# The gates of the routing stage by token halves, with part of the path weighting moved between them

## What is computed

```python
outs = [local_out, mid_out, delta_out, v_direct]
...
router_feat = jnp.concatenate([hidden_states] + feats, axis=-1)
h1 = jax.nn.silu(router_feat @ r_w1 + r_b1)
logits = (h1 @ r_w2 + r_b2).reshape(B, L, H, 4)
p = jax.nn.softmax(logits, -1)
p = p * (1.0 - 4.0 * FLOOR) + FLOOR
mixed = sum((p[..., i:i + 1] * outs[i] for i in range(4)))
rms = jnp.sqrt(jnp.mean(mixed * mixed, -1, keepdims=True) + EPS_MIX)
mixed = mixed / rms * mix_w
```

## Time and profile before

| | us |
|---|---|
| median of three runs | 8313.55 (8311.75 to 8318.34) |
| time of the profiled execution | 8321.09 |
| its span, first to last instruction | 8319.4 |
| TensorE busy | 7418.7 (89%) |
| VectorE busy | 4851.6 (58%) |
| ScalarE busy | 3369.7 (41%) |
| mean granted TensorE clock | 0.942 of full speed |

### The profile page before, as it was taken

One profiled execution on the slowest core, in us unless ns is written; L12 is line 12 of the kernel. 1 busy time (PEld: TensorE's weight loads), 2 busy tenths in 40 slices (PEclk: granted clock), 3 DMA queues, 4 the chain that ended last, 5 costly groups with the idle time before them and its releaser, 6 DMA issues. The chain is left out here.

```text
span 8319.4 us, 123018 instructions
## 1 busy us (share of the span) xinstructions
PE 7418.7 (89%) x48014; PEld 4312.9 (52%) x48014; DVE 4851.6 (58%) x9364; ACT 3369.7 (41%) x6883; POOL 1774.6 (21%) x2690
## 2 busy tenths in 40 slices
PE   6899988999889898899898998988999889998898
PEld 3546455464554645546455464554645546455464
DVE  5465654656646566565665646656466564666546
ACT  2252432525325253352533525335253442534425
POOL 2212221122211212112221122211222121221121
PEclk9999999999999999999999999999999999999999
DMA  3021210112112021120211202112021210212102
GB/s 73 18 34 28 37 41 21 33 25 37 41 23 43 13 37 41 28 40 15 32 41 29 39 15 32 41 34 44 6 32 41 37 41 6 32 41 37 41 10 33
DMA packets 337771, 268.59 MB, mean 32 GB/s; under 512 B 213521, under 2 KB 276369, under 8 KB 337097
## 3 DMA queue, kind: packets, MB, share of 16 engines
q1 hardware_dynamic: 337148, 260.09, 16.7%
HBM read 48.71 MB, written 42.02 MB: 11 GB/s over the span
## 5 line engine op out<-in xcount | busy, mean ns | idle before, releaser
L1814 DVE TENSOR_REDUCE sa_nm<-ps 128x2 f32<-128x1024 f32 (+4 forms) x1280 | 1393.5, 1115 | 388.9 <-PE ps L1799 198.5
L1889 ACT ACTIVATE pre<-ps 128x512 f32<-128x512 f32 (+3 forms) x3072 | 1272.3, 491 | 743.3 <-PE ps L1877 737.8
L1877 PE MATMUL ps<-sa_qs,sa_ks 99*128 99x512 bf16 (+3 forms) x3072 | 806.8, 337 | 136.6 <-DMA sa_qs<-sa_mrow 72.6
L1795 PE MATMUL ps<-sa_ks,sa_qs 96*128 96x512 bf16 (+3 forms) x2560 | 660.6, 332 | 82.8 <-DVE sa_nm L1814 68.9
L1896 POOL TENSOR_SCALAR_AFFINE_SELECT pre<-pre 128x512 f32<-128x512 f32 x512 | 325.0, 635 | 1766.6 <-ACT pre L1889 1764.2
L1909 PE MATMUL ps<-pre,sa_va 128*17 128x512 f32 (+3 forms) x6144 | 644.8, 491 | 8.2 <-POOL pre L1896 8.2
L1877 PEld LDWEIGHTS ps<-sa_qs,sa_ks 99*128 99x128 bf16 x3072 | 259.3, 98 | 715.8 <-ACT pre L1889 473.8
L318 PE MATMUL ps<-identb 128*128 128x512 bf16 x2320 | 583.2, 398 | 10.5 <-ACT dr_z L1153 10.5
L705 PE MATMUL ps<-rep,stack 128*32 128x512 f32 x4608 | 530.9, 613 | 33.7 <-DMA rep<-paths 33.7
L949 POOL TENSOR_TENSOR A<-paths 128x256 f32<-128x256 f32 x384 | 268.0, 726 | 792.3 <-DVE paths L1119 792.3
L1795 PEld LDWEIGHTS ps<-sa_ks,sa_qs 96*128 96x128 bf16 x2560 | 248.8, 101 | 269.0 <-DVE sa_nm L1814 98.5
(11 more groups left out here) (364 smaller groups left out, 14154.2 us busy)
## 6 DMA issues: line engine op xcount, KB each, us to landing
sa_qs<-sa_parts SPq DMA_DIRECT2D x288, 128.0 KB, 4.5
sa_ks<-sa_parts SPq DMA_DIRECT2D x288, 128.0 KB, 5.9
x<-in_x SPq DMA_DIRECT2D x17, 1024.0 KB, 5.6
rep<-paths SPq DMA_DIRECT2D x128, 128.0 KB, 2.7
bounce<-paths SPq DMA_DIRECT2D x32, 512.0 KB, 2.9
out_y<-x SPq DMA_DIRECT2D x32, 512.0 KB, 3.0
rep<-paths SPq DMA_DIRECT2D x128, 127.9 KB, 2.6
rep<-paths SPq DMA_DIRECT2D x128, 127.8 KB, 3.4
```

Of the source, the lines that this page charges most:

```text
L1795: last = nc.tensor.matmul(cols[:, i, :], qs[0:NCOMB * AD, g % NBUF, op.j + i, op.t * P:(op.t + 1) * P], ks[0:NCOMB * AD, g % NBUF, op.j + ...
L1814: nc.vector.tensor_reduce(nm[:, g % 2, op.c, op.t, op.j:op.j + op.heads], cols, AX.X, ALU.max, negate=True).then_inc(s.slot_free, 1)
L1877: last = nc.tensor.matmul(bank[:, off:], ks[0:QROWS, g % NBUF, j, kt * P:(kt + 1) * P], qs[0:QROWS, g % NBUF, j, n * BANK + off:(n + 1) * ...
L1889: nc.scalar.activation(pt[:, gs % 2, j, off:BANK], ring_bank(ring_use(gs, j))[:, off:], ACT.Exp, scale=RATIO).then_inc(s.ring_out, 1)
```

## The change

The softmax is made for one token half at a time, on VectorE and on ScalarE. `gather_logits_of(0)` moves up, behind unit 7 instead of behind unit 9, and raises `logits` for its half. After the first half's gates VectorE weights paths 0 to 2 of that half inside `route`, then copies the second half's partial logits, weights path 3 of the first half, and makes the second half's gates. A new semaphore, `read`, tells TensorE that the first half's logits have been read from their PSUM bank. In `mix_and_project` only the second half's four weightings remain, and `mix(0, ...)` waits for none. The diff, cut to its core:

```diff
+def weigh_path(nc, m, i, n):
+
+    tn, gn = T // NB, T * H // NB
+    path = (m.local_tm, m.mid_tm, m.delta_tm, m.v_tm)[i][:, n * tn:(n + 1) * tn, :].rearrange("p t (h d) -> p (t h) d", h=H)
+    return nc.vector.tensor_tensor(path, path, m.prob[:, n * gn:(n + 1) * gn, i:i + 1].to_broadcast([P, gn, DH]), ALU.mult)
...
-                act.wait_ge(s.shifted, 1)
-                nc.scalar.activation(lg[:].rearrange("p n c -> p (n c)"), lg[:].rearrange("p n c -> p (n c)"),
-                                     ACT.Exp).then_inc(s.exp, 1)
+                for n in range(NB):
+                    act.wait_ge(s.shifted, n + 1)
+                    nc.scalar.activation(lg[:, groups(n), :], lg[:, groups(n), :], ACT.Exp).then_inc(s.exp, 1)
...
                 for n in range(NB):
+                    tiles, half = slice(n * (BANK // P), (n + 1) * (BANK // P)), groups(n)
                     dve.wait_ge(s.partial_ps, n + 1)
                     nc.vector.tensor_copy(partial[:, n * BANK:(n + 1) * BANK], ps[:, PARTIAL[n], :]).then_inc(s.partial, 1)
...
+                    if n:
+                        weigh_path(nc, m, PATHS - 1, 0)
+                    dve.wait_ge(s.logits, n + 1)
...
+                    dve.wait_ge(s.read, n + 1)
+                    settle(nc.vector.tensor_reduce(red[:, half], lg[:, half, :], AX.X, ALU.max))
+                    nc.vector.tensor_tensor(lg[:, half, :], lg[:, half, :], bc(red[:, half], PATHS), ALU.subtract).then_inc(s.shifted, 1)
+                    dve.wait_ge(s.exp, n + 1)
...
+                    gates = nc.vector.tensor_scalar(m.prob[:, half, :], lg[:, half, :], 1.0 - PATHS * FLOOR, FLOOR, ALU.mult, ALU.add)
+                    if n == 0:
+                        settle(gates)
+                        for i in range(PATHS - 1):
+                            weigh_path(nc, m, i, 0)
...
                 def gather_logits_of(n):
                     pe.wait_ge(s.partial, n + 1)
+                    if n:
+                        pe.wait_ge(s.read, n)
...
-                    return last
+                    last.then_inc(s.logits, 1)
...
                     if u == HC + 1:
                         partial_logits_of(0)
-                gather_logits_of(0)
+                    if u == HC + 2:
+                        gather_logits_of(0)
                 partial_logits_of(1)
-                gather_logits_of(1).then_inc(s.logits, 1)
+                gather_logits_of(1)
...
-                for n in range(NB):
-                    for i in range(PATHS):
-                        nc.vector.tensor_tensor(of(paths[i], n), of(paths[i], n),
-                                                m.prob[:, n * GN:(n + 1) * GN, i:i + 1].to_broadcast([P, GN, DH]),
-                                                ALU.mult).then_inc(s.part, 1)
+                for i in range(PATHS):
+                    weigh_path(nc, m, i, 1).then_inc(s.part, 1)
...
-                        pe.wait_ge(s.part, PATHS * n + i + 1)
+                        if n:
+                            pe.wait_ge(s.part, i + 1)
```

More of the change, by code:

```diff
@@ L1191, in route, with groups @@
         partial = sb("ro_partial", [P, L])
+        def groups(n):
+            return slice(n * (T * H // NB), (n + 1) * (T * H // NB))
         def feature(first, n):
@@ new lines, in _ @@
+                    dve.wait_ge(s.logits, n + 1)
+                    nc.vector.tensor_tensor(lg[:, half, :].rearrange("p (t h) c -> p t (h c)", h=H),
+                                            ps[:, 6, 0:T * H * PATHS].rearrange("p (t n) -> p t n", t=T)[:, tiles],
+                                            k.rb2[:].unsqueeze(1).to_broadcast([P, BANK // P, H * PATHS]), ALU.add).then_inc(s.read, 1)
+                    dve.wait_ge(s.read, n + 1)
+                    settle(nc.vector.tensor_reduce(red[:, half], lg[:, half, :], AX.X, ALU.max))
@@ new lines, in _ @@
+                    nc.vector.tensor_tensor(lg[:, half, :], lg[:, half, :], bc(red[:, half], PATHS), ALU.subtract).then_inc(s.shifted, 1)
+                    dve.wait_ge(s.exp, n + 1)
+                    settle(nc.vector.tensor_reduce(red[:, half], lg[:, half, :], AX.X, ALU.add))
+                    settle(nc.vector.reciprocal(red[:, half], red[:, half]))
+                    settle(nc.vector.tensor_tensor(lg[:, half, :], lg[:, half, :], bc(red[:, half], PATHS), ALU.mult))
+                    gates = nc.vector.tensor_scalar(m.prob[:, half, :], lg[:, half, :], 1.0 - PATHS * FLOOR, FLOOR, ALU.mult, ALU.add)
@@ L2169 @@
           "x_ps x10 t01 t23 y6_ps y6 t_ps t6 kq attn ks r u_ps u s_ps state o o_out",
-    "ro": "feats ft_ps ft h1_ps h1 partial_ps partial logits shifted exp",
+    "ro": "feats ft_ps ft h1_ps h1 partial_ps partial logits read shifted exp",
     "mi": "part mixed square kept summed scale_in scale wide spread ot out",
```

## The result

The changed kernel is slower: 8395.04 us median against 8315.94, a ratio of 1.0089 (95% interval 1.0073 to 1.0105). That is 79 us or 4.9 us for each of 16 sequences, where 43 us had been forecast (2.7 a sequence), and above the range, which ended at 8384. The profiled execution has a span of 8393.0 against 8319.4, 4.6 us a sequence.

What follows compares the result with a forecast made beforehand. TensorE, busy 89% of the span, was taken as the bound, so gains must come from its idle time. Terms 1.65 + 0.2 + 0.4 + 0.45 gave 2.7 us for each of 16 sequences, +43 us: 8356, range 8326 to 8384.

Steps and rivals of the forecast that it cites:

- Steps 1 to 3: First half's gates in routing: last Silu 1.11 us later, Exp done at 287.32, VectorE reaches first weighting at 288.38.
- step 1: Gathering of the first half ahead of units 8 and 9: the last Silu ends 1.11 us later.
- Step 4: Three weightings ahead of the second copy on VectorE, 3.44 us: the copy ends 3.35 us later.
- Steps 6 to 8: Second half's gates take 2.03 us, mix starts net 1.65 later; two sequences lose their fast partial logits, averaged +0.2.
- Step 9: Second gathering on TensorE, after a longer idle time, runs at a lower clock: +0.4 us, bounds nothing and +1.1.
- steps 1 to 9: Everything up to the start of the mix: 1.65 + 0.2 + 0.4 us later in each sequence.
- Step 10: Mix restarts at clock 0.50 with a low stretch at least as long: +0.45 us, bounds -1.9 and +2.0.
- A: The terms as summed: +43 us, 8356, own range 8335 to 8370; chance 0.60.
- D: Low stretch of the mix twice as long and second gathering slow: 4.9 us a sequence, +79 us, 8393; chance 0.22.
- B: Clock stays at 1.00 across the gap before the mix, saving 1.9 us: 8313, half of it 8328; chance 0.13.
- C: Second copy isn't held up by the three weightings and the kernel is faster, 8302 to 8271; chance 0.05.
- step 2: First half's Exp on ScalarE waits for ten Silus and a 1.28 us table load, ending at 287.32.

Runs made afterwards that it cites:

- both edits: Changed kernel with paths 2 and 3 weighted in the mix block, one weighting before the second copy, first gathering behind the last unit: 8355.80 us, ratio 1.0044.

## Why the prediction was wrong

**Bound and prize (what bounds the kernel).** Right: TensorE's gap ahead of the mix, of which moving weightings could take 1.28 us. They took it: the mix starts with its block.

**Steps 1 to 3.** Right. The last Silu ends 4.64 us behind the first copy (forecast 4.57), the Exp of the first half at 6.21 (6.09), with no pause behind the table load, and the first weighting starts at 7.27 (7.15). The run with the gathering late shows the chain from step 1 on. The further 1.38 us that I had worked out from the Trainium skill, ScalarE: Activation LUTs, section "What ACT_TABLE_LOAD costs", didn't appear here either: the load ends at 286.32 and the Exp starts at 286.33.

**Step 4, the queue.** Right: second copy at 10.68, forecast 10.59. The run with the copy early takes 2.7 us off the start of the mix.

**Steps 6 to 8.** Right: 2.06 us of gates (2.03), 0.30 for the meeting, and the two fast sequences have lost their lead, all 16 start the mix at 15.7 to 16.0.

**Step 9, clock of the second gathering.** Right mechanism, wrong size: 1.89 instead of 1.07 us, 0.8 where I took 0.4. The weighting beside it had ended by 292.9, 0.8 before the logits, and hid nothing of the excess. With this the start of the mix is 2.69 later against 2.25 forecast in steps 1 to 9 (1.65 + 0.2 + 0.4).

**Step 10, clock of the mix.** This term failed: 0.45 us taken, 1.61 measured. I took it for one low stretch at the start of the mix. There it grew from 4.0 to 5.2 us in the first sequence, which costs 0.6 us. But there is a second low stretch, at the spreading of the scales, that the working never looked at. Before it lasts 3.4 us in all 16 sequences; after the change it lasts 6.8 in six of them. One of these, the second, with its spreading and projection:

```profile
840.80:847.50 6.70, 6.05 (x26) 5.58 (x26) 2.67 (x4) 1.05 (x1) 1.14 (x1) 0.50 0.01 2
```

The six average 43.22 us from mix to feed-forward, the other ten 41.26, against 40.39 before: 0.87 more in every sequence, some 0.6 of which the longer first stretch explains, and 0.73 on the average of all from the six. The changed kernel with fillings, at 38.79 us, shows that the clock holds the whole excess of this term and more. My own bound of +2.0 would have held it.

**A term that the sum lacked.** I let the effect of the change end with the feed-forward's first matmul. The rest took 0.54 us more a sequence. In 13 of the 16 sequences a low stretch lies at the start of the routing stage, in five before, and each such sequence takes 1.7 us longer from its first hidden matmul to the first copy (30.87 instead of 29.17). Two sequences of the kernel before, without and with it:

```profile
767.30:796.50 29.20, 28.95 (x73) 10.21 (x74) 1.41 (x10) 5.88 (x9) 0.00 (x0) 1.00 0.00 1
1284.05:1314.95 30.90, 30.65 (x73) 10.80 (x74) 1.42 (x10) 5.89 (x9) 0.00 (x0) 0.94 0.00 1
```

This is 0.79 us a sequence, of which 0.25 is won back in the stages between. That the change brings these stretches isn't shown: the first sequence's routing stage has one in the trace after and none in the trace before, though no changed instruction stands ahead of it. The cause of this term stays open. Sum: 2.69 + 1.61 + 0.54 = 4.8 us a sequence, against 2.7.

**The rivals.** A had the mechanism, D the size: the result lies at D's full price, 8393. The closeness is partly luck, for D's two clock terms, 2.0 and 1.1, measured 1.61 and 0.8, and the term that the sum lacked made up most of the difference. I had given D 0.22 and yet closed the range half way to it, at 8384. B fell, for the clock was at 0.50 at the start of all 16 mixes. C fell with step 2.

The Trainium skill, TensorE: Matmul & The Clock Gate, section "HAM oscillation — how this bites in real kernels", describes a matmul kernel whose bursts start cold behind each wait. This trace agrees, with 0.50 in the first 5.2 us of the mix; with the wait filled, the mix starts at 1.00.

## What to carry to other kernels

VectorE took its queue in order: the copy's input was ready at 288.7, and the copy ran at 291.06, behind three weightings. So work that is free where an engine idles isn't free ahead of the copy that another engine waits for: set the short, waited-for instruction first and fill behind it. The delay in front of TensorE cost more than its length here, 1.4 times (36 us of delay, 52 of time), and an earlier start gained nothing as long as the clock fell in the gaps. Price each place where the clock is low behind the change, not only the nearest, or take the clock out of the comparison with filling matmuls before judging an order, and look whether the fillings themselves hold anything up.

## What the runs showed of the hardware that I had not expected

- 21 filling matmuls a sequence, whose result nobody reads, made the kernel before 0.57% faster (8273.08), more than any reordering; its mix runs in 10.98 us instead of 12.81.
- Starting the mix 1.3 us earlier went with a mixing stage 2.3 us longer (both edits), and 1.74 us of lead were lost over the rest of the sequence even with full clock in the mixing stage.
- In the kernels without fillings the second low stretch of the mixing stage was 3.4 us long where the first ended at most 5.39 us behind the start of the mix, and 6.8 where it ended at 5.47 or later. A sequence with the long one took some 2 us more from mix to feed-forward (43.22 against 41.26 in the changed kernel).
- Gathering with 16 columns on TensorE takes 1.89 us at half clock and 1.07 at full.
